# Two-layer FFN with adapters in float32: paired loads of down tiles, scale factors split once, second adapter factors prepared earlier

## The reference

```python
def _L0_cond_ref(x, W_gate, W_up, W_down, A_gate, B_gate, ..., lora_indices, layer_idx):
    gate = lora_add(x @ W_gate.T, x, A_gate, B_gate)      # F = 1376 inner columns, rank 16 adapters, chosen per sequence
    up   = lora_add(x @ W_up.T, x, A_up, B_up)
    act  = silu(gate) * up
    return lora_add(act @ W_down.T, act, A_down, B_down)  # lora_add(base, inp, A, B) = base + 0.5 * (inp @ A.T) @ B.T
def _L0_ffn_ref(x, ...):                                  # I = 1792, every weight is w * (su @ sv), su and sv of rank 4
    return lin(silu(lin(x, gate)) * lin(x, up), down)
x = x + _L0_ffn_ref(_L0_cond_ref(x, ...), ...)
x = x + _L1_ffn_ref(_L1_cond_ref(x, ...), ...)            # a linear layer with adapters, then an FFN with int4-like weights
```

## Time and profile before

| what | value |
|---|---|
| time, median of 3 runs | 631.68 us (631.31 to 633.65) |
| the profiled execution: its own time | 630.1 us |
| its span, first to last instruction | 628.5 us |
| PE busy | 606.4 us (96%), 2904 matmuls |
| DVE busy | 481.1 us (77%) |
| ACT busy | 297.0 us (47%) |
| POOL busy | 298.8 us (48%) |
| mean granted TensorE clock | 0.986 of full speed |
| DMA | 55.88 MB, mean 89 GB/s |

### The profile page before, as it was taken

One profiled execution on the slowest core, in us unless ns is written; L12 is line 12 of the kernel. 1 busy time (PEld: TensorE's weight loads), 2 busy tenths in 40 slices (PEclk: granted clock), 3 DMA queues, 4 the chain that ended last, 5 costly groups with the idle time before them and its releaser, 6 DMA issues.

```text
span 628.5 us, 8117 instructions
## 1 busy us (share of the span) xinstructions
PE 606.4 (96%) x2904; PEld 494.0 (79%) x2904; DVE 481.1 (77%) x597; ACT 297.0 (47%) x418; POOL 298.8 (48%) x226
## 2 busy tenths in 40 slices
PE   8999859999997989999999999999999999999997
PEld 7777648788775868888888888888788888888886
DVE  6797747676865899977436878746689998999988
ACT  4755114334332354453112545425548887478860
POOL 6565035124514104683022658360003788958897
PEclk9999969999998999999999999999999999999999
DMA  7873690254034202411213111151233212321203
GB/s 245 213 204 60 173 246 14 76 134 118 13 84 128 70 27 67 168 30 59 64 33 100 34 34 30 59 116 34 80 101 100 64 58 64 101 67 64 62 27 134
DMA packets 29580, 55.88 MB, mean 89 GB/s; under 512 B 10149, under 2 KB 13605, under 8 KB 29221
## 3 DMA queue, kind: packets, MB, share of 16 engines
q1 hardware_dynamic: 27716, 52.51, 28.9%
q0 software_dynamic: 1536, 2.33, 1.7%
q10 hardware_dynamic: 288, 0.52, 0.2%
HBM read 48.47 MB, written 5.84 MB: 86 GB/s over the span
## 4 chain that ended last, share of the span: by engine, by line
PE 82%; DVE 7%; DMA 6%; issue 1%; ACT 1%; SPq 1%; POOL 1%; POOLq 0%; DVEq 0%
PE ps_down L2381 5%; PE ps_down L2382 5%; PE ps_down L2383 5%; PE ps_gate L2650 3%; PE ps_gate L2649 3%; PE ps_up L2649 3%; PE ps_up L2650 3%; PE ps_m L2649 3%; PE ps_m L2650 3%; PE ps_down L2649 3%; PE ps_down L2650 3%; PE ps_gate L2489 3%; PE ps_gate L2491 3%; PE ps_gate L2490 3%; PE ps_up L2489 2%; PE ps_up L2490 2%
## 5 line engine op out<-in xcount | busy, mean ns | idle before, releaser
L1132 POOL TENSOR_TENSOR up_sum<-up_sum,up_more 128x1024 f32<-128x1024 f32 x14 | 33.7, 2407 | 62.0 <-DVE up_more L1945 62.0
L1091 POOL TENSOR_TENSOR act_lo<-up,act_hi 128x512 fp32r<-128x512 f32 x14 | 18.2, 1298 | 68.0 <-ACT act_hi L1456 68.0
L2381 PE MATMUL ps_down<-act_hi,w_hi 128*128 128x512 f32 x112 | 43.9, 392 | 0.0
L1011 POOL TENSOR_TENSOR cond_total<-w_raw 128x512 f32<-128x512 f32 x8 | 11.2, 1396 | 68.6 <-DMA w_raw<-in_cond_gu 38.2
L2382 PE MATMUL ps_down<-act_lo,w_hi 128*128 128x512 f32 x112 | 43.6, 390 | 0.0
L2383 PE MATMUL ps_down<-act_hi,w_lo 128*128 128x512 f32 x112 | 43.6, 389 | 0.0
L1945 DVE SCALAR_TENSOR_TENSOR gate_sum<-ps_up,s_group,gate_sum 128x1024 f32<-128x1024 f32 x28 | 35.8, 1280 | 3.6 <-PE ps_up L2650 3.6
L1688 DVE TENSOR_TENSOR w_lo<-w_total,w_hi 128x512 fp32r<-128x512 f32 (+1 forms) x28 | 28.0, 1000 | 13.3 <-ACT w_hi L1450 12.9
L1144 POOL TENSOR_TENSOR act_lo<-gate_sum,act_hi 128x1024 fp32r<-128x1024 f32 x14 | 33.7, 2417 | 6.3 <-DVE gate_sum L1953 6.3
L1450 ACT ACTIVATE w_hi<-w_total 128x512 fp32r<-128x512 f32 (+1 forms) x28 | 20.7, 738 | 30.1 <-POOL w_total L1085 19.3
L2204 DVE TENSOR_TENSOR xp<-xp,ps_down 128x512 f32<-128x512 f32 x20 | 13.6, 684 | 27.4 <-PE ps_down L2383 27.4
(11 more groups left out here) (424 smaller groups left out, 2057.0 us busy)
## 6 DMA issues: line engine op xcount, KB each, us to landing
w_int<-in_ffn_gu SPq DMA_DIRECT2D x14, 512.0 KB, 3.6
w_raw<-in_cond_gu SPq DMA_DIRECT2D x9, 512.0 KB, 6.0
w_raw<-in_ffn_gu SPq DMA_DIRECT2D x9, 512.0 KB, 3.5
w_raw<-in_ffn_dn SPq DMA_DIRECT2D x8, 448.0 KB, 3.2
w_int<-in_ffn_dn SPq DMA_DIRECT2D x8, 448.0 KB, 3.3
b_rows<-b_split SPq DMA_DIRECT2D x12, 256.0 KB, 4.8
xp<-in_x SPq DMA_DIRECT2D x8, 256.0 KB, 5.0
w_raw_third<-in_ffn_gu SPq DMA_DIRECT2D x4, 512.0 KB, 3.6
```

Source lines behind the costliest of these rows:

```text
L1132: nc.gpsimd.tensor_tensor(up_sum[:, u % 3, :], up_sum[:, u % 3, :], up_more[:, u % 2, :], ALU.add).then_inc(up_done, 1)
L2381: nc.tensor.matmul(ps[:, :], weights_hi[:, cols], rhs_hi(k), start=start and n == 0, stop=False)
```

## The change

Four things change.

1. Down tiles of cond are loaded in pairs, two tiles into the two halves of one raw slot (`load_down`, `halves_raw`, `tile_raw`): two transfers where there were four. A slot is therefore free for another use earlier, and ffn0's tile 0 now takes a slot of `w_raw` (`load_seven(phases[6], 0)`), issued ahead of the read of the adapters' low parts (`fill(filled_lo, 1)`); `w_raw_first` is gone.
2. The scale factors come in one transfer of 96 rows, are split once (one ScalarE and one VectorE instruction over 288 columns), stored to DRAM by six DMAs and read back spread by 18 (`store_factors`, `spread_factors`) after GpSimd has zeroed the targets. The twelve instructions of pack on VectorE are gone.
3. b rest has a buffer of its own (in the place of pack), so that its eight loads need not wait for tile 3; ScalarE splits it before the end of tile 3, VectorE in down a.
4. In down c VectorE makes the low parts of the masked adapter rows before `first_product`, ffn0's pieces move behind the eviction of o = 0, the sum x6 moves from GpSimd to VectorE, and the product of ffn0's tile 1 moves behind the eviction of o = 1. In down a and b the pieces of the next gate/up tile stand first.

```diff
+
+def halves_raw(layer, kind):
+
+    return (layer, kind) == ("cond", "down")
 
...
+            if halves_raw(ph.layer, ph.kind):
+                slot = (ph.s0 + j // 2) % 2
+                if j % 2:
+                    raw[ph.name, j] = raw[ph.name, j - 1]
+                    holder[slot] = ph.t0 + j
                     continue
...
-        b_raw = [place("b_raw0", [P, B_FIRST], F32, at["lora_b1"]), place("b_raw1", [P, B_REST], F32, ring)]
...
+        b_raw = [place("b_raw0", [P, B_FIRST], F32, at["lora_b1"]), place("b_raw1", [P, B_REST], F32, at["pack"])]
...
-        b_hi_rest = [place("b_hi1", [P, B_CUT], F32R, ring + 4 * B_REST), place("b_hi2", [P, B_REST - B_CUT], F32R, at["w"] + 12 * KB)]
+        b_hi_rest = place("b_hi1", [P, B_REST], F32R, at["xp"] + 7 * KB)
...
+            def load_down(ph, pair):
+
+                here, n = raw_of[ph.name, 2 * pair], full_columns(ph)
+                sp.wait_ge(w_ready, here.before)
+                both = w_raw[:, here.slot, :].rearrange("p (o n) -> p o n", o=2)
+                first, second = (d[name][2 * pair:2 * pair + 2].rearrange("o p n -> p o n") for name in ("cond_dn_a", "cond_dn_b"))
+                early = max(0, min(n, (CUT - ph.first) * P))
+                late = max(0, ph.first - CUT) * P
+                if early:
+                    sp.dma_start(both[:, :, 0:early], first[:, :, ph.first * P:ph.first * P + early]).then_inc(raw_in[here.slot], 16)
+                if early < n:
+                    sp.dma_start(both[:, :, early:n], second[:, :, late:late + n - early]).then_inc(raw_in[here.slot], 16)
...
-            sp.wait_ge(pack_zero, 2)
-            for q in range(4):
-                for v in range(4):
-                    row = 32 * q + SR * v
-                    sp.dma_start(pack_raw[row:row + SR, :], d["factors"][min(q, 2)]).then_inc(pack_in, 16)
-            load(down_a, 0)
-            load(down_a, 1)
-            sp.wait_ge(cond_seven, cond_step(3, "u1"))
             for b in range(BC, NB):
                 load_b(sp, b, indices[b], 1, b_rest_in[b // BC])
-            load(down_a, 2)
...
+            sp.dma_start(factor_raw[:, :], d["factors"].rearrange("n r (q c) -> (n r q) c", c=FACTOR_COLS)).then_inc(factor_in, 16)
...
+            def store_factors(value, half):
+
+                for n in range(3):
+                    sp.dma_start(factor_split[n, half * SR:(half + 1) * SR, :].rearrange("r (q c) -> (r q) c", c=FACTOR_COLS),
+                                 value[quarter(n), :].bitcast(F32)).then_inc(factor_stored, 16)
+
+            def spread_factors(n):
+
+                long, short = factor_split[n, :, 0:F1], factor_split[n, :, F1:PACK]
+                for part in range(2):
+                    row = PR * n + 2 * SR * part
+                    sp.dma_start(pack_long[row:row + 2 * SR, :].bitcast(F32), long).then_inc(pack_in, 16)
+                for row in range(0, 4 * SR, SR):
+                    to, half = PR * n + row, row // (2 * SR)
+                    sp.dma_start(pack_short[to:to + SR, n, :].bitcast(F32), short[half * SR:(half + 1) * SR, :]).then_inc(pack_in, 16)
...
             spread_b(2)
-            load(gu_b, 1)
             load(gu_b, 2)
-            load(down_b, 0)
-            load(down_b, 1)
+            sp.wait_ge(pack_zero, 2)
+            sp.wait_ge(factor_stored, 16 * 6)
+            for n in range(3):
+                spread_factors(n)
...
             sp.wait_ge(tail_stored, 16 * 2)
             sp.wait_ge(cond_seven, cond_step(9, "7"))
             fill(filled_hi, 0)
+            load_seven(phases[6], 0)
             sp.wait_ge(cond_seven, cond_step(NKD - 1, "u1"))
             fill(filled_lo, 1)
-            sp.dma_start(w_raw_first[:, :], d["ffn0_gu"][0]).then_inc(first_raw_in, 16)
-            for o in range(2, HK):
...
-            pool.wait_ge(t_sums, CH)
-            pool.wait_ge(cond_x_summed, 5)
-            nc.gpsimd.memset(pack_raw[:, :], 0.0).then_inc(pack_zero, 1)
...
+            for b in range(BC):
+                load_b(pool, b, indices[b], 1, b_rest_in[b // BC])
...
-            pool.wait_ge(cond_seven, cond_step(3, "u1"))
-            for b in range(BC):
-                load_b(pool, b, indices[b], 1, b_rest_in[b // BC])
             cond_sums(4)
+            pool.wait_ge(b_stored[3], 16)
+            nc.gpsimd.memset(pack_long[:, :].bitcast(F32), 0.0).then_inc(pack_zero, 1)
+            nc.gpsimd.memset(pack_short[:, :, :].bitcast(F32), 0.0).then_inc(pack_zero, 1)
             cond_sums(5)
...
             def cond_down(ph):
 
                 t = COND_FIRST[ph.part + 1]
-                if ph.part == 0:
-                    tile_hi(ph, 1, 0)
-                    hi_of_b_rest()
-                    cond_piece(t, 0)
-                else:
-                    tile_hi(ph, 1, 0)
-                    cond_piece(t, 0)
+                cond_piece(t, 0)
+                tile_hi(ph, 1, 0)
+                cond_piece(t, 1)
                 tile_hi(ph, 1, 1)
-                for piece in (1, 2):
-                    cond_piece(t, piece)
+                cond_piece(t, 2)
...
 
                 t = COND_FIRST[ph.part + 1]
-                if ph.part == 0:
-                    pack_long_factors()
+                cond_piece(t, 0)
                 cond_evict(ph, 0)
                 tile_lo(ph, 1, 0)
                 if ph.part == 0:
-                    pack_short_factors()
+                    lo_of_b_rest()
+                    dve.wait_ge(b_ready, 3)
+                    dve.wait_ge(b_stored[2], 16)
+                    dve.wait_ge(factor_stored, 16 * 6)
+                cond_piece(t, 1)
                 cond_evict(ph, 1)
-                if ph.part == 0:
-                    lo_of_b_rest()
-                cond_piece(t, 0)
                 tile_lo(ph, 1, 1)
+                cond_piece(t, 2)
                 cond_evict(ph, 2)
-                for piece in (1, 2):
-                    cond_piece(t, piece)
                 cond_evict(ph, 3)
...
+                    lo_of_t_down()
                     first_product()
-                    lo_of_t_down()
-                    first_weights(named["ffn0 gate/up a"])
                     return
...
-                    if ph.name == "cond down c" and o == 1:
-                        tile_product(nxt, 0, 1, ps_ups)
...
-                    if ph.name == "cond1" or o == 0:
+                    if ph.name == "cond1":
                         if o == 2:
                             last_weights_lo()
                         down_tile(ph, o)
+                    elif o == 0:
+                        down_tile(ph, o)
+                        first_weights(nxt)
                     elif o == 1:
                         down_tile(ph, o)
+                        x_sum(6, None)
                         x_low(2, None)
+                        x_low(6, None)
                         piece_lo(nxt, 0, 2)
+                        tile_product(nxt, 0, 1, ps_ups)
                     elif o == 2:
                         down_tile(ph, o, (0,))
                         x_sum(4, 0)
-                        x_low(6, None)
...
                             t_down(NKD - 1)
-                            pe.wait_ge(pack_ready, 2)
+                            pe.wait_ge(pack_in, 16 * 18)
```

186 lines of the change are left out of this document (70 added, 116 removed).

## The result

| | kernel before | changed kernel |
|---|---|---|
| median of 4 runs each, in turn on one chip | 631.49 us (629.65 to 633.65) | 613.22 us (612.23 to 614.44) |
| ratio, with its 95% interval | | 0.971 (0.967 to 0.975) |
| span of the profiled execution | 628.5 us | 611.2 us |
| TensorE busy | 606.4 us | 601.7 us |

The forecast was 613.9 us. A later measurement of the changed kernel, on another occasion, gave 613.09 against 630.97 (ratio 0.972, 0.970 to 0.974). The span fell by 17.3 us; the sum of the prediction was 17.8.

What follows compares the result with a forecast made beforehand. TensorE, busy 606.4 of 628.5 us, bounds the kernel, with idle time mostly in part a and down c. Terms +1.5 - 9.5 - 1.4 - 0.4 - 8.0 = -17.8 gave 612.3, or 613.9 us as median; 8-of-10 range 610.5 to 620.5.

Steps and rivals of the forecast that it cites:

- The long wait in part a: Part a, down tile 3's low part: gate/up tile 4 issued near 59, 18 us earlier, removes the wait, -9.5 us.
- its slow matmuls: Part a, behind the long wait: seven matmuls near half speed return to full speed, -1.4 us.
- `cond_e`: End of tile 3: one tiny pack instruction ahead instead of six takes 0.4 of the 0.6 us wait.
- The start: Early b rest loads in the full DMA stretch delay the `b_rows`: +1.5 us, bounds 0 and 4.
- The rule of turns between queues: Start: an engine alternates between queues, so GpSimd's loads would hold up the first `b_rows`, upper half of 0 to 4 us.
- the rule on 16 partitions: Start: limited port bandwidth would land the pair of down tiles 1 to 1.5 us later, sum up to 1 us worse.
- Down c: Earlier ffn0 tile 0 load and masked rows done first let VectorE's unbroken run start earlier: -8.0 us, between 6.7 and 9.2.
- the rival that gave the order alone: Down c, late ffn0 load: only the masked rows' move helps, about 3 of 8 us; 619 us, chance 0.07.
- The sum: Whole kernel: +1.5 - 9.5 - 1.4 - 0.4 - 8.0 = -17.8 us against the profiled execution's 630.1.
- The forecast's own range: Whole kernel: 610.5 to 616.5 us, from start 0 to 4 and down c 6.7 to 9.2; chance 0.57.
- The start costs more: Rival, start: early loads delay `b_rows` and tile 3's sums, ScalarE waits for b rest; 617 to 619 us, chance 0.2.
- The slot doesn't free early enough: Rival, down c: ffn0's tile 0 loads late again, VectorE's run begins as before; 619 us, chance 0.07.

Runs made afterwards that it cites:

- a5: Changed kernel, load of gate/up tile 4 held until TensorE finished down tiles 0 and 1 of part a, 11.3 us later: 621.47 us (0.9864).
- a2: Changed kernel, GpSimd's copy of the down factors a and its four b rest loads held for the third low part of x: 610.63 us (0.9682).
- a1: Changed kernel, GpSimd's sums of gate/up tile 7 held until the low part of tile 6's activations is written: 610.83 us (0.9685).
- b1: Kernel before with only the order changed, low parts of the masked adapter rows ahead of the first product: 629.97 us (0.9985).
- d2: Changed kernel with only the load undone, ffn0's raw tile 0 issued behind the fill of the adapters' low parts: 614.10 us (0.973).
- a3: Changed kernel, GpSimd's four b rest loads issued after the sums of gate/up tile 3: 614.58 us (0.9735).
- c0: Changed kernel unaltered, timed again as a reference: 613.09 us.
- d1: Changed kernel with only the order undone, low parts of the masked adapter rows behind the first product: 615.29 us (0.977).
- e1: Changed kernel with the sum 6 of x back on GpSimd: 615.25 us (0.977).
- a4: Changed kernel, load of gate/up tile 4 held until TensorE finished down tile o = 0 of part a, 6 us later: 612.71 us (0.9711).

## Why the prediction was right, and where its steps were wrong

- **The long wait in part a, -9.5, and its slow matmuls, -1.4.** Right: -9.65 and -1.45 by the table of matmuls. The chain came out as forecast: b rest's high part at 51.3, the load at 58.41, in use from 62.58, the low part at 71.10 to 71.79 against a need at 76.3, 4.5 us of margin. a5 shows that this load is the cause. One thing in the step was wrong: down tile 3 is not what is late next, down tile 2 is. The six factor stores took 4.55 us and not 2.2, under cover.
- **`cond_e`, -0.4.** -0.8 between the second `b_rows` and the start of down a; the 0.6 us wait is gone whole, and with it the slow restart of one matmul.
- **The start, +1.5.** Too high: +0.64 at the second `b_rows`, with a wait of 0.5 for `cond_lo` and one of 0.2 for `b_rows` itself in it. The first `b_rows` (33.27 against 33.41) was not delayed. GpSimd's loads came at 32.34 and not at 31, since its copy waited for its own input until 29.76. The transfers did slip, by 2.8 us (7.3 against 4.5), but slack took all but 0.2; the 0.5 came from the copy that the same edit let GpSimd start 4.5 us earlier, into VectorE's sums. So the term was mis-sized, and over half of the waiting has another cause than the one given. The rule of turns between queues, cited from the Trainium skill's "DMA: Bandwidth & Descriptors" for the upper half of the bounds, did not cost what that half assumed, since the first `b_rows` was not held up. Whether the queues took turns over the later ones stays open: in the changed kernel GpSimd's queue moved 36 packets from 36.0 to 37.0 us and SyncE's 2, though in the kernel before the `b_rows`, issued 0.4 us later, moved at that time; a2 says little on it, as the two queues hardly met there. Nor was the pair of down tiles late, as the rule on 16 partitions, cited from the Trainium skill's "SBUF — State Buffer", would have had it: ScalarE started on it at 50.25, before the 52 of the forecast.
- **Nothing was priced in part b.** Here a step is missing. The prediction said of the moved loads of ffn0 that they cost nothing, and did not follow the same freed slots to gate/up tile 7, whose load came 21 us earlier and whose sums then ran beside VectorE: +1.9 us by the table (-11.23 to -9.33), of which the wait is 1.8, shown by a1. The rows for it were there, in the 3.03 against 1.22 us of the earlier trace rows.
- **Down c, -8.0.** -8.1 (from -9.33 to -17.43), and the run began at 190.34; 199.8 less the 9.33 by which part b had shifted is 190.5. The masked rows ran at 181.48 (190.8 less 9.33 is 181.5) in 2.29 us. But why VectorE could start then was told incompletely. It needed the product of ffn0's tile 1 out of its way too, as b1 shows; the sentence that tile 1's load costs nothing holds only with that move (argued from the order and from b1, not run alone). And the rival that gave the order alone "about 3 of 8 us" was too generous: it gives 0.9.
- **The sum** was right by 0.5 us (-17.8 against -17.3) because two misses of nearly one size had opposite signs. The start was 0.9 us too dear, `cond_e` 0.4 and the other terms 0.3 too small, which makes 1.5 too slow, and 1.9 us were missing in part b. That they cancel is luck. The forecast's own range, 610.5 to 616.5, does not follow from its terms either: a start of 0 to 4 and a down c of 6.7 to 9.2 give 611.2 to 617.7.
- **The rivals.** None came true. "The start costs more" was right that the transfers slip and wrong that TensorE would see it. "The slot doesn't free early enough" would have cost 1.2 us (d2) and not 5: the order covers for the load.

## What to carry to other kernels

Where a change frees a buffer early (a memory area that the next load waits for), follow every load that waited for it to the engine that works on it first, and ask what runs beside that work: here sums on GpSimd, 20 us earlier than before and 9 us earlier than the work around them, cost TensorE 1.8 us, and one wait on GpSimd won it back. When a wait disappears, look for the next load in the same engine's queue before counting the gain; b1 won 7.3 us at one place and kept 0.9. Two edits that cover for each other must be undone together to be priced.

## What the runs showed of the hardware

- VectorE can lose to GpSimd several times in one instruction: with four instructions of GpSimd back to back, a product of 0.69 us took 4.05 (a3); one started just behind a sum took 1.72. GpSimd can lose as well: its copy of the down factors took 2.40 us in a2 and 4.10 in a3, where VectorE ran low parts back to back beside it at their usual length (0.69). GpSimd's memset of 2.03 us in the kernel before slowed nothing: the two low parts of VectorE beside it took 2.35 together, and 2.36 in a2, which has no memset there.
- The granted clock after a wait of about 1.9 us is not the same each time. The same wait at the start of down b, 1.9 us in both, left it at 1.00 in c0 and was followed by 7 matmuls at 0.50 (1.2 GHz) in a3:

```profile
119.20:122.20 3.00, 2.47 (x11) 2.06 (x12) 3.00 (x6) 0.73 (x2) 0.00 (x0) 1.00 0.50 102
```

```profile
121.20:124.20 3.00, 3.00 (x7) 2.36 (x8) 1.88 (x4) 0.09 (x1) 0.00 (x0) 0.50 0.28 56
```

  That cost a3 another 1.6 us. In b1 too a wait of 1.9 us was followed by half speed (0.52 from 203.2 to 206.2 us). What decides it was not tried. It may be why runs of one kernel fall into two groups (a3, d1, e1), but of each only one run was profiled.
- SyncE's stores from 32 partitions took longer to issue than its store from 128: the three of `factor_hi` 2.99 us, 1.0 each, beside 0.34 for the store of b rest's high part just ahead of them; the three of `factor_lo` 0.52 each, and 0.72 in a4. Whether this is the stores or the queue that was full was not told apart.
